# Attention probabilities split in fp16 with three products each, and the softmax maximum taken from the stacked 128-row operands

## The chip, the cores and the metric

The kernel runs on one core of a Trainium2 chip. The metric is the device time of one launch in microseconds (us). TensorE multiplies matrices, VectorE (DVE in the profile), ScalarE (ACT) and GpSimd (POOL) do the element-wise work, and SyncE (SP) issues the transfers (DMA). Every engine runs its own list of instructions in order and waits on semaphores that others raise.

## The reference, cut to what matters

Two layers, each a cross attention followed by a mixture of experts, on x of 2 x 1024 x 256 tokens. The change lies in the first attention alone. There the queries are the layer-normalised x (with 2 x 1024 rows), keys and values come from 77 context rows and the 1024 normalised tokens together:

```
q = latn @ Wq;  kv = concatenate([xn, latn]) @ Wkv      # 16 heads of 64
weight = softmax(einsum('bhld,bhnd->bhln', q * scale, k * scale))
out = einsum('bhln,bhnd->bhld', weight, v);  out @ Wo
```

So for each of 2 batches and 16 heads there are scores of 1024 queries against 1101 keys, an exponential of each, a product with values, and a division by the row's sum.

## The kernel before, in words

Every fp32 quantity that goes into a product is split into an upper part and a remainder, and three products (upper upper, upper remainder, remainder upper) are added.

**Turns and steps.** The first attention works in 16 turns (`turn`, one for a pair of heads, 8 pairs for each of 2 batches). A turn has STEPS = 36 steps: 2 heads x 2 halves of 512 queries x KT = 9 tiles of up to 128 keys. All engines walk through the same steps in their own `turn` functions, and the order of everything in a step is written out by hand.

**A step on TensorE** (`turn`, line 1621) is: the scores of the step three ahead (AHEAD = 3; `scores`, two matmuls of 512 columns, L1582 and L1583, into one of two score banks), and the product of this step's probabilities and values (`attend`, L1602: four groups of 128 queries, with four matmuls of 65 columns each). The scores for a bank need the exponentials of the step two before to be done (s_exp). ScalarE takes one exponential of the 512 columns (L810) into PT, which is fp32. The upper part of a probability is read in place: `upper` takes the upper 16 bits of the fp32 word as bf16. GpSimd (L642) or VectorE (L1104, in the ten VECTOR_STEPS) subtracts it from PT and stores the fp16 remainder PR. `attend` waits for that remainder.

**Stacked operands.** For the scores, Q and K of a head are copied by DMA into stacks: QA holds the upper part of Q twice (2 x 64 rows), KA the upper part and the remainder of K, QB the remainder of Q and a 65th row with minus the maximum of each query, KB the upper part of K and a row of ones. `stack_head` on the SP queue (L505, L508) issues six such transfers for a head, each of about 256 to 276 KB. For head 1 it waits for the first scores of the turn (s_score), for head 0 of the next turn for the last split of the next turn's K (s_jobfree). Each transfer adds 16 to s_stack of its head, so a full stack adds 96.

**The maximum.** The 65th row of QB needs the maximum of each query's scores first. For eight tiles of 128 queries, `max_part` (L1532) makes approximate scores from the upper parts alone: per tile a matmul of 512 keys into the first maximum bank (a = 0, before `attend`), and after `attend` one of 78 and one of 512 keys (a = 1; L1538, L1540). It reads Q and K of the head, 64 rows each, straight from where they were split, not from the stack. VectorE reduces each bank (L1032, L1036); `max_part` waits for the reduction of the tile before (s_mxfree). Then the maxima are joined, turned by TensorE (`max_turn`, M1_T and M0_T), negated, and sent by a small DMA into the row of QB.

**What lies on which step.** Head 1's maxima lie at steps 1 to 8 (M1_AT = 1), head 0's of the next turn at 19 to 26 (M0_AT = 19). Turning the attention output of the turn before lies at steps 1 and 2, its output product at 3 to 6, the projection of the next turn's Q and K (`project_qk`, five jobs) at 13 to 17 (QK_AT = 13). In this text, a step with a tile of maxima is a maximum step; there are 16 in a turn, and 20 plain ones.

**First batch's first head.** Its maxima are taken between the value projections (`values`), which wait for the split of Q and K alone.

Of the kernel before, what the change touches and what calls it, by code (L numbers as in the profile page):

```python
# [7 lines left out]

# [1 line left out]

# [3 lines left out]
P = 128  # L16
ALU = mybir.AluOpType
ACT = mybir.ActivationFunctionType
AX = mybir.AxisListType
F32 = mybir.dt.float32  # L20
F32R = mybir.dt.float32r
U32 = mybir.dt.uint32
BF16 = mybir.dt.bfloat16
F16 = mybir.dt.float16
RMAX = bass.bass_isa.ReduceOp.max

B, T, D = 2, 1024, 256
S = 77
SP = S + 1
NC = D // P  # L30
NT = B * T // P
TB = T // P
HD = 64
PAIRS = 1024 // P
KT = TB + 1
NK = T + SP
NKP = NK + 2
HALF = 512
EPS = 1e-5
STEPS = 4 * KT  # L40
RING = 6
AHEAD = 3
JOBS = 12
VJOBS = 2 * KT
MAX0_T = 2 * TB
BOUND_AT = 9
WQK0_AT = 5
QK0_AT = 9
AWJOBS = 6
# [15 lines left out]
def program(nc, x, ctx, ln1w, ln1b, ln2w, ln2b, wqk0, wv0, wo0, wr, rbias, w1, b1, w2, b2, gb,  # L65
            watt, bqk1, bvo1, wgu, wd, convw, convb, out):
    stack = ExitStack()
    with stack:
# [3 lines left out]
        def sem(name):  # L72
            return stack.enter_context(nc.semaphore(name))
# [3 lines left out]
        score_banks = [ps[:, 0, :], ps[:, 1, :]]  # L77
        max_banks = ps[:, 2:4, :].rearrange("p a n -> p (a n)")
        small_bank = ps[:, 4, :]
# [16 lines left out]
        def sb0(name, shape, dt=F32):  # L96
            return st0.enter_context(nc.sbuf_tensor(name, shape, dt))
# [2 lines left out]
        C = sb0("C", [P, B, D])  # L100
        lnp = sb0("lnp", [P, 4, NC])
        lat = {k: sb0("lat_" + k, [P, B, NC, NKP], F32R) for k in "hl"}
        latf = sb0("latf", [P, 2, HALF])
        wqk_raw = sb0("wqk_raw", [P, NC, 2, P])
        wo_raw = sb0("wo_raw", [P, D])
        wqk = {k: sb0("wqk_" + k, [P, NC, 2, P], F32R) for k in "hl"}
# [1 line left out]
        Q = {k: sb0("Q_" + k, [P, T], F32R) for k in "hl"}  # L108
        K = {k: sb0("K_" + k, [P, NKP], F32R) for k in "hl"}

        QA = [sb0(f"QA{h}", [P, T], F32R) for h in range(2)]
        QB = [sb0(f"QB{h}", [P, T], F32R) for h in range(2)]
        KA = [sb0(f"KA{h}", [P, NKP], F32R) for h in range(2)]
# [2 lines left out]
        V = {k: sb0("V_" + k, [P, KT, 2 * PAIRS, HD + 1], F16) for k in "hl"}  # L116
        PT = sb0("PT", [P, RING, HALF])
        PR = sb0("PR", [P, RING, HALF], F16)
        AT = sb0("AT", [P, TB, P])
        with ExitStack() as early:  # L120
            wv_raw = early.enter_context(nc.sbuf_tensor("wv_raw", [P, NC, KT * P - P], F32))
# [117 lines left out]
        s_wvh = sem("wv_rounded")  # L239
        s_wqk, s_wv, s_wo = sem("wqk_split"), sem("wv_split"), sem("wo_split")  # L240
        s_bounds, s_bound, s_vs = sem("bounds_by_partition"), sem("bounds_ready"), sem("value_scale_ready")
        s_rem_pool, s_rem_dve = sem("remainders_by_gpsimd"), sem("remainders_by_vector")
        s_job = sem("shared_bank_full")
        s_cast = sem("shared_bank_rounded")
# [9 lines left out]
        s_exp = sem("exp_done")  # L254
# [138 lines left out]
            return shared[(1 + idx) % 2]  # L393

        def upper(s):
            return PT[:, s % RING, :].bitcast(BF16).rearrange("p (n two) -> p n two", two=2)[:, :, 1]


        VECTOR_STEPS = (2, 11, 13, 15, 17, 19, 29, 31, 33, 35)

        def on_vector(s):
            return s in VECTOR_STEPS
# [51 lines left out]


        A_AT, WO_AT = 1, 3
        M1_AT, M1_MAX, M1_T = 1, 9, 12
        QK_AT, M0_AT, M0_MAX, M0_T = 13, 19, 27, 29
        WQK_AT, WO_SPLIT_AT = 9, 16

        UNITS = GR * FC
        UP_AHEAD = 2
# [296 lines left out]
        def _(act):  # L759
# [3 lines left out]
                nc.scalar.copy(dst, bk[:, 0:SP] if j == 4 else bk).then_inc(s_cast, 1)  # L763

            act.wait_ge(s_in, 16 * 6)
            for k, (b, c, h) in enumerate(LATJOBS):
                act.wait_ge(s_lat_full, k + 1)
                n = HALF if h < 2 else SP
                w = 2 if h < 2 else 0
                nc.scalar.activation(lat["h"][:, b, c, HALF * h:HALF * h + n], shared[k % 2][:, 0:n], ACT.Identity,  # L770
                                     bias=lnp[:, w + 1, c:c + 1], scale=lnp[:, w, c:c + 1]).then_inc(s_lat_hi, 1)
                if k == WQK0_AT:
                    act.wait_ge(s_wqk_raw, 16)
                    nc.scalar.copy(flat(wqk["h"]), flat(wqk_raw)).then_inc(s_wqk, 1)
                if k >= QK0_AT:
                    round_qk(k - QK0_AT, k - QK0_AT, first_qk_bank(k - QK0_AT))
# [28 lines left out]
            def turn(b, i, g, nb):  # L805
                for s in range(STEPS):
                    m = P if s % KT < TB else S
                    act.wait_ge(s_score, STEPS * g + s + 1)
                    act.wait_ge(s_pv, STEPS * g + s + 1)
                    nc.scalar.activation(PT[0:m, s % RING, :], score_banks[s % 2][0:m], ACT.Exp,  # L810
                                         scale=HD ** -0.5).then_inc(s_exp, 1)
                    at = s - AHEAD
                    if at >= 0 and at % KT == KT - 1:
                        u = at // KT
                        act.wait_ge(s_pv, STEPS * g + at + 1 + RING)
                        act.wait_ge(s_norm, 4 * g + u + 1)
                        nc.scalar.copy(PVS[:, u % 2], pv_bank).then_inc(s_pvc, 1)
                    if A_AT <= at < A_AT + 2:
                        att_hi(jobs_before(b, i), at - A_AT)
                    if nb is not None and QK_AT <= at < QK_AT + 5:  # L820
                        if at == QK_AT:
                            act.wait_ge(s_stack[1], 96 * g + 96)
                        j = at - QK_AT
                        round_qk(j, jobs_before(b, i) + AWJOBS + j, bank(AWJOBS + j))
# [123 lines left out]
        def _(dve):  # L948
# [5 lines left out]
            dve.sem_inc(s_norm, 2)  # L954
            for h in range(2):
                nc.vector.memset(KB[h][HD:HD + 1, :].bitcast(F32), 1.0).then_inc(s_const, 1)
            dve.wait_ge(s_in, 16 * 6)
            dve.wait_ge(s_const, 8)

# [537 lines left out]
        def _(pe):  # L1497
# [34 lines left out]
            def max_part(h, t, a, n):  # L1532

                pe.wait_ge(s_mxfree, 2 * n + a + 1)
                r = slice(HD * h, HD * h + HD)
                q = Q["h"][r, t * P:t * P + P]
                if a == 1:
                    nc.tensor.matmul(small_bank[:, t % 4 * SP:t % 4 * SP + SP], q, K["h"][r, T:NK],  # L1538
                                     start=True, stop=True)
                nc.tensor.matmul(max_banks[:, a * HALF:a * HALF + HALF], q, K["h"][r, a * HALF:a * HALF + HALF],  # L1540
                                 start=True, stop=True).then_inc(s_mx, 1)

            def max_tile(h, t, n):
# [7 lines left out]
            def values(b, job):  # L1551

                for j in range(VJOBS):
                    kt, half = divmod(j, 2)
                    m = P if kt < TB else S
                    pe.wait_ge(s_jobfree, job + j + 1)
                    product(shared[(job + j) % 2][0:m],
                            [(lat[u][:, b, c, kt * P:kt * P + m], wv[v][:, c, HALF * half:HALF * half + HALF])
                             for c in range(NC) for u, v in RANDL]).then_inc(s_job, 1)
                    if b == 0 and half == 0 and kt < TB:  # L1560
                        if kt == 0:
                            pe.wait_ge(s_jobfree, 5 + 2)
                        max_tile(0, kt, kt)
                    if b == 0 and j == MAX0_T:
                        max_turn(0)
# [20 lines left out]
            def attend(g, pair, s):  # L1586
                h, kt = s // (2 * KT), s % KT
                m = P if kt < TB else S
                if on_vector(s):
                    pe.wait_ge(s_rem_dve, len(VECTOR_STEPS) * g + by_vector(s))  # L1590
                else:
                    pe.wait_ge(s_rem_pool, (STEPS - len(VECTOR_STEPS)) * g + s + 1 - by_vector(s))
                if kt == 0:
                    pe.wait_ge(s_pvc, 4 * g + s // KT + 1)
                head = 2 * pair + h
                vh, vl = ((V[k][0:m, kt, head, :] if isinstance(head, int) else
                           V[k][0:m, kt, bass.ds(head, 1), :].squeeze(1)) for k in "hl")
                for q in range(4):
                    c = slice(q * P, q * P + P)
                    for k, (p, v) in enumerate(((upper(s)[0:m, c], vh), (upper(s)[0:m, c], vl),  # L1600
                                                (PR[0:m, s % RING, c], vh), (PR[0:m, s % RING, c], vl))):
                        mm = nc.tensor.matmul(pv_bank[:, q, :], p, v, start=(kt == 0 and q == 0 and k == 0),  # L1602
                                              stop=(kt == KT - 1 and k == 3), skip_group_check=True)
                mm.then_inc(s_pv, 1)

            def att_turn(job, j, bk):
# [14 lines left out]
            def turn(b, i, g, nb):  # L1621
                job = jobs_before(b, i)
                last = i == PAIRS - 1
                for s in range(STEPS):
# [4 lines left out]
                    if M1_AT <= s < M1_AT + TB:  # L1629
                        if s == M1_AT:  # L1630
                            pe.wait_ge(s_maxrow, 2 * g + 1)
                        max_part(1, s - M1_AT, 0, 16 * g + 8 + s - M1_AT)
                    if nb is not None and M0_AT <= s < M0_AT + TB:
                        if s == M0_AT:
                            pe.wait_ge(s_jobfree, job + AWJOBS + 5 + 2)
                            pe.wait_ge(s_maxrow, 2 * g + 2)
                        max_part(0, s - M0_AT, 0, 16 * g + 16 + s - M0_AT)
                    if A_AT <= s < A_AT + 2:
# [401 lines left out]
```

## Time and profile before

| | us |
|---|---|
| three runs | 2375.3, 2377.93 (median), 2394.89 |
| profiled execution | 2373.98 |
| its span, first to last instruction | 2372.3 |
| TensorE matmul busy | 2243.4 (95%) |
| VectorE, GpSimd, ScalarE busy | 1282.3, 1121.8, 728.2 |
| mean granted TensorE clock | 0.949 |

The first attention runs from about 60 us to 1190 us of the span, then the experts of layer 0 to about 1980 us, then layer 1. The busy time of TensorE counts matmuls from start to modelled end, and they overlap, so the distance from one start to the next tells what a matmul costs the engine. A granted clock of 1.00 is 2.4 GHz, and 0.50 is 1.2 GHz.

### The profile page before, as it was taken

How to read it: one execution, taken by the hardware profiler on the slowest of the kernel's cores; microseconds unless marked ns; L12 is line 12 of the kernel's file. 1: busy time of each engine (PE TensorE's matmuls, PEld its weight loads, DVE VectorE, ACT ScalarE, POOL GpSimd, SP SyncE). 2: the span in 40 equal slices, each digit the busy share in tenths (PEclk: the TensorE clock that was granted, in tenths of full speed). 3: DMA queues.
4: the chain of work that ended last, by engine and by line, in shares of the span. 5: the costliest groups of instructions: out<-in, count | busy, mean ns of one | idle time of the engine just before them, and what ended most of it. 6: DMA issues, size and time to landing. Idle time of an engine off the chain costs nothing.

```text
span 2372.3 us, 47010 instructions
## 1 busy us (share of the span) xinstructions
PE 2243.4 (95%) x19460; PEld 1684.1 (71%) x19460; DVE 1282.3 (54%) x2444; ACT 728.2 (31%) x1227; POOL 1121.8 (47%) x1102
## 2 busy tenths in 40 slices
PE   2999999999999999999959999999999997899888
PEld 2666666666666666666639998998998986556567
DVE  8656655666556655565653333333333369535586
ACT  2343333333343344333432222222221221112222
POOL 4144444444335444444536676666665655112132
PEclk9999999999999999999979999999999998657699
DMA  1222222122112222122120000001000000000000
GB/s 63 63 63 45 48 64 58 41 64 63 32 35 64 63 64 62 35 59 64 32 80 19 19 21 34 19 19 37 19 19 19 18 1 0 1 1 1 22 16 27
DMA packets 31026, 87.23 MB, mean 37 GB/s; under 512 B 6820, under 2 KB 13796, under 8 KB 28389
## 3 DMA queue, kind: packets, MB, share of 16 engines
q1 hardware_dynamic: 30820, 84.25, 14.4%
q8 instruction: 158, 2.59, 0.4%
q14 instruction: 48, 0.39, 0.1%
HBM read 29.76 MB, written 2.10 MB: 13 GB/s over the span
## 4 chain that ended last, share of the span: by engine, by line
PE 89%; DVE 6%; issue 1%; ACT 1%; POOL 1%; DMA 0%; POOLq 0%; ACTq 0%; DVEq 0%
PE ps L1504 29%; PE ps L1754 15%; PE ps L1602 13%; PE ps L1582 8%; PE ps L1540 8%; PE ps L1583 6%; PE ps L1846 5%; PE ps L1538 2%; DVE Y L358 1%; PE ps L1609 1%; PE ps L1824 1%; DVE stats L339 1%; PE ps L1694 0%; POOL ln_tmp L376 0%; PE ps L1848 0%
## 5 line engine op out<-in xcount | busy, mean ns | idle before, releaser
L642 POOL TENSOR_TENSOR PR<-PT 128x512 f16<-128x512 f32 (+1 forms) x416 | 445.1, 1072 | 607.0 <-ACT PT L810 606.7
L810 ACT ACTIVATE PT<-ps 128x512 f32<-128x512 f32 (+1 forms) x576 | 344.0, 598 | 537.9 <-PE ps L1583 537.9
L1032 DVE TENSOR_REDUCE mxs<-ps 128x1 f32<-128x512 f32 x512 | 352.3, 689 | 219.9 <-PE ps L1540 219.9
L685 POOL TENSOR_TENSOR h_l<-hf,h_h 128x512 fp32r<-128x512 f32 x256 | 336.4, 1315 | 244.6 <-DVE hf L1206 238.6
L1206 DVE TENSOR_SCALAR hf<-ps,b1e 128x512 f32<-128x512 f32 x256 | 191.7, 750 | 447.0 <-ACT h_h L882 446.2
L882 ACT ACTIVATE h_h<-ps,b1e 128x512 fp32r<-128x512 f32 x256 | 176.0, 688 | 563.0 <-PE ps L1504 562.9
L1602 PE MATMUL ps<-V_h,PT 128*128 128x65 f16 (+1 forms) x2304 | 329.7, 197 | 5.0 <-POOL PR L642 4.0
L1602 PEld LDWEIGHTS ps<-V_h,PT 128*128 128x128 bf16 (+1 forms) x2304 | 225.5, 98 | 150.2 <-issue 134.9
L1602 PE MATMUL ps<-V_l,PT 128*128 128x65 f16 (+1 forms) x2304 | 324.1, 194 | 0.0
L1602 PE MATMUL ps<-V_l,PR 128*128 128x65 f16 (+1 forms) x2304 | 321.9, 194 | 0.0
L1602 PE MATMUL ps<-V_h,PR 128*128 128x65 f16 (+1 forms) x2304 | 321.4, 193 | 0.0
L1754 PE MATMUL ps<-w_h,h_h 128*128 128x256 f32 x1024 | 291.6, 285 | 3.1 <-POOL h_l L685 3.0
L1754 PE MATMUL ps<-w_l,h_h 128*128 128x256 f32 x1024 | 290.1, 283 | 0.0
L1754 PE MATMUL ps<-w_h,h_l 128*128 128x256 f32 x1024 | 290.1, 283 | 0.0
L1582 PE MATMUL ps<-QA,KA 128*128 128x512 f32 (+1 forms) x576 | 273.9, 476 | 2.6 <-DMA QB<-maxT 2.1
L1540 PE MATMUL ps<-K_h,Q_h 64*128 64x512 f32 x512 | 248.1, 486 | 0.0
L1602 PEld LDWEIGHTS ps<-V_l,PT 128*128 128x128 bf16 (+1 forms) x2304 | 227.7, 99 | 0.4
L1583 PE MATMUL ps<-QB,KB 65*128 65x512 f32 (+1 forms) x576 | 227.9, 396 | 0.0
L1602 PEld LDWEIGHTS ps<-V_h,PR 128*128 128x128 f16 (+1 forms) x2304 | 226.5, 98 | 0.0
L1602 PEld LDWEIGHTS ps<-V_l,PR 128*128 128x128 f16 (+1 forms) x2304 | 224.7, 98 | 0.0
L1504 PE MATMUL ps<-XT_h,w_h 128*128 128x512 f32 x512 | 203.1, 397 | 7.1 <-DVE hf L1206 4.7
L1754 PEld LDWEIGHTS ps<-w_h,h_h 128*128 128x128 f32 x1024 | 195.7, 191 | 17.3 <-POOL h_l L685 4.1
(307 smaller groups left out, 4560.2 us busy)
## 6 DMA issues: line engine op xcount, KB each, us to landing
QA<-Q_h SPq DMA_DIRECT2D x64, 256.0 KB, 3.4
w_raw<-w SPq DMA_DIRECT2D x16, 1024.0 KB, 4.8
KA<-K_h SPq DMA_DIRECT2D x32, 275.5 KB, 5.2
KA<-K_l SPq DMA_DIRECT2D x32, 275.5 KB, 5.4
KB<-K_h SPq DMA_DIRECT2D x32, 275.5 KB, 5.6
QB<-Q_l SPq DMA_DIRECT2D x32, 256.0 KB, 4.3
wqk_raw<-wqk SPq DMA_DIRECT2D x16, 256.0 KB, 3.9
wo_raw<-wo SPq DMA_DIRECT2D x18, 128.0 KB, 4.5
```

Of the source, the lines that this page charges most:

```text
L642: nc.gpsimd.tensor_tensor(PR[0:m, s % RING, :], PT[0:m, s % RING, :], upper(s)[0:m], ALU.subtract).then_inc(s_rem_pool, 1)
L685: nc.gpsimd.tensor_tensor(hs["l"][:, u % 4], hf[:, u % 2], hs["h"][:, u % 4].bitcast(F32), ALU.subtract).then_inc(s_hlo, 1)
L810: nc.scalar.activation(PT[0:m, s % RING, :], score_banks[s % 2][0:m], ACT.Exp, scale=HD ** -0.5).then_inc(s_exp, 1)
L882: nc.scalar.activation(hs["h"][:, u % 4], hidden_banks[u % 2], ACT.Relu, bias=b1e[:, k, u % FC:u % FC + 1]).then_inc(s_hhi, 1)
L1032: r = nc.vector.reduce_max(mxs[:, a, t:t + 1], max_banks[:, a * HALF:a * HALF + HALF], AX.X)
L1206: nc.vector.tensor_scalar(hf[:, u % 2], hidden_banks[u % 2], b1e[:, k, u % FC:u % FC + 1], 0.0, ALU.add, ALU.max).then_inc(s_hf, 1)
L1504: mm = nc.tensor.matmul(o, l, r, start=(k == 0), stop=(k == n - 1), **kw)
L1540: nc.tensor.matmul(max_banks[:, a * HALF:a * HALF + HALF], q, K["h"][r, a * HALF:a * HALF + HALF], start=True, stop=True).then_inc(s_mx, 1)
L1582: nc.tensor.matmul(o, KA[h][:, k], QA[h][:, q], start=True, stop=False)
L1583: nc.tensor.matmul(o, KB[h][0:HD + 1, k], QB[h][0:HD + 1, q], start=False, stop=True) \
L1602: mm = nc.tensor.matmul(pv_bank[:, q, :], p, v, start=(kt == 0 and q == 0 and k == 0), stop=(kt == KT - 1 and k == 3), skip_group_check=True)
L1754: mm = nc.tensor.matmul(o, hs[a][:, u % 4, t * P:t * P + P], w2s[b][:, k, f, :], start=(f == 0 and j == 0 and t % 2 == 0), stop=(f == FC - ...
```

## The change

- The exponential is multiplied by 1024 (a bias `lift` = 10 ln 2, read from a column of SBUF), and is taken twice by ScalarE from the same score bank: once as fp32 into PT, once as fp16 into a new buffer PU. `upper` returns PU. The semaphore for "exponential done" is raised by the second.
- `attend` drops the product of the remainder of the probabilities with the remainder of the values: three matmuls for each of the four groups, not four.
- `max_part` reads QA and KA of the head, 128 rows, not 64 rows of Q and K. It therefore waits for the stack: head 1's first tile for s_stack[1], head 0's for s_stack[0] of the next turn, and the one in `values` for the first stack of all.
- Places move: the maxima of head 1 from steps 1-8 to 3-10, their turn from 12 to 13, the projections of the next turn from 13-17 to 10-14, the split of their weights on GpSimd from step 9 to 7; head 0's maxima stay at 19-26. VECTOR_STEPS has ten entries as before, at other places.

```diff
-MAX0_T = 2 * TB
+MAX0_T = 2 * TB + 1
...
         def upper(s):
-            return PT[:, s % RING, :].bitcast(BF16).rearrange("p (n two) -> p n two", two=2)[:, :, 1]
-        VECTOR_STEPS = (2, 11, 13, 15, 17, 19, 29, 31, 33, 35)
+            return PU[:, s % RING, :]
+        VECTOR_STEPS = (2, 14, 16, 18, 19, 20, 30, 32, 34, 35)
...
-        M1_AT, M1_MAX, M1_T = 1, 9, 12
-        QK_AT, M0_AT, M0_MAX, M0_T = 13, 19, 27, 29
-        WQK_AT, WO_SPLIT_AT = 9, 16
+        M1_AT, M1_MAX, M1_T = 3, 11, 13
+        QK_AT, M0_AT, M0_MAX, M0_T = 10, 19, 27, 29
+        WQK_AT, WO_SPLIT_AT = 7, 16
...
                     nc.scalar.activation(PT[0:m, s % RING, :], score_banks[s % 2][0:m], ACT.Exp,
-                                         scale=HD ** -0.5).then_inc(s_exp, 1)
+                                         bias=lift[0:m, 0:1], scale=HD ** -0.5)
+                    nc.scalar.activation(PU[0:m, s % RING, :], score_banks[s % 2][0:m], ACT.Exp,
+                                         bias=lift[0:m, 0:1], scale=HD ** -0.5).then_inc(s_exp, 1)
...
                 pe.wait_ge(s_mxfree, 2 * n + a + 1)
-                r = slice(HD * h, HD * h + HD)
-                q = Q["h"][r, t * P:t * P + P]
+                q = QA[h][:, t * P:t * P + P]
                 if a == 1:
-                    nc.tensor.matmul(small_bank[:, t % 4 * SP:t % 4 * SP + SP], q, K["h"][r, T:NK],
+                    nc.tensor.matmul(small_bank[:, t % 4 * SP:t % 4 * SP + SP], q, KA[h][:, T:NK],
                                      start=True, stop=True)
-                nc.tensor.matmul(max_banks[:, a * HALF:a * HALF + HALF], q, K["h"][r, a * HALF:a * HALF + HALF],
+                nc.tensor.matmul(max_banks[:, a * HALF:a * HALF + HALF], q, KA[h][:, a * HALF:a * HALF + HALF],
                                  start=True, stop=True).then_inc(s_mx, 1)
...
                         if kt == 0:
-                            pe.wait_ge(s_jobfree, 5 + 2)
+                            pe.wait_ge(s_stack[0], 96)
...
                     for k, (p, v) in enumerate(((upper(s)[0:m, c], vh), (upper(s)[0:m, c], vl),
-                                                (PR[0:m, s % RING, c], vh), (PR[0:m, s % RING, c], vl))):
+                                                (PR[0:m, s % RING, c], vh))):
...
                         if s == M1_AT:
                             pe.wait_ge(s_maxrow, 2 * g + 1)
+                            pe.wait_ge(s_stack[1], 96 * g + 96)
...
                         if s == M0_AT:
-                            pe.wait_ge(s_jobfree, job + AWJOBS + 5 + 2)
+                            pe.wait_ge(s_stack[0], 96 * g + 192)
```

## Rows read from the trace of the kernel before

**Rows 1.** The page: granted clock in 40 slices of the span, and VectorE's reductions.
```profile
PEclk9999999999999999999979999999999998657699
...
L1032 DVE TENSOR_REDUCE mxs<-ps 128x1 f32<-128x512 f32 x512 | 352.3, 689 | 219.9 <-PE ps L1540 219.9
```

**Rows 2.** Timeline of TensorE's matmuls, a plain step: start us, duration us, instruction.
```profile
339.76 0.48 PE L1582 MATMUL ps<-QA,KA 128*128 128x512 f32 x1
340.08 0.40 PE L1583 MATMUL ps<-QB,KB 65*128 65x512 f32 x1
340.32 0.21 PE L1602 MATMUL ps<-V_h,PT 128*128 128x65 f16 x1
...
340.82 0.48 PE L1582 MATMUL ps<-QA,KA 128*128 128x512 f32 x1
```

**Rows 3.** Timeline of TensorE's matmuls, a maximum step of head 0.
```profile
343.05 0.50 PE L1582 MATMUL ps<-QA,KA 128*128 128x512 f32 x1
343.38 0.39 PE L1583 MATMUL ps<-QB,KB 65*128 65x512 f32 x1
343.70 0.50 PE L1540 MATMUL ps<-K_h,Q_h 64*128 64x512 f32 x1
344.13 0.21 PE L1602 MATMUL ps<-V_h,PT 128*128 128x65 f16 x1
...
344.73 0.30 PE L1538 MATMUL ps<-K_h,Q_h 64*128 64x78 f32 x1
344.86 0.48 PE L1540 MATMUL ps<-K_h,Q_h 64*128 64x512 f32 x1
345.27 0.50 PE L1582 MATMUL ps<-QA,KA 128*128 128x512 f32 x1
```

**Rows 4.** Timeline of TensorE's matmuls, 128-row products behind one another.
```profile
335.70 0.39 PE L1582 MATMUL ps<-QA,KA 128*128 128x512 f32 x1
335.93 0.39 PE L1583 MATMUL ps<-QB,KB 65*128 65x512 f32 x1
...
338.13 0.39 PE L1582 MATMUL ps<-QA,KA 128*128 128x512 f32 x1
...
339.65 0.28 PE L1504 MATMUL ps<-lat_h,wqk_l 128*128 128x78 f32 x1
```

**Rows 5.** Timeline of ScalarE: exponentials, a cast, an activation with a bias column.
```profile
308.37 0.60 ACT L810 ACTIVATE PT<-ps 128x512 f32<-128x512 f32 x1 [1.11 <-PE ps L1583]
311.39 0.60 ACT L810 ACTIVATE PT<-ps 128x512 f32<-128x512 f32 x1 [2.42 <-PE ps L1583]
...
335.90 0.59 ACT L763 CAST K_h<-ps 128x512 fp32r<-128x512 f32 x1 [1.35 <-PE ps L1504]
336.38 0.60 ACT L810 ACTIVATE PT<-ps 128x512 f32<-128x512 f32 x1
...
1890.56 0.69 ACT L882 ACTIVATE h_h<-ps,b1e 128x512 fp32r<-128x512 f32 x1 [2.47 <-PE ps L1504]
1891.14 0.61 ACT L887 CAST wa_h<-w_raw 128x512 fp32r<-128x512 f32 x1
```

**Rows 6.** Timeline of the SP queue: stacks of heads 1, 0 and 1.
```profile
298.52 1.11 SPq L505 DMA_DIRECT2D QA<-Q_h  x2
...
340.50 1.14 SPq L505 DMA_DIRECT2D QA<-Q_h  x2
...
344.88 1.40 SPq L508 DMA_DIRECT2D KB<-K_h  x1
...
365.66 1.11 SPq L505 DMA_DIRECT2D QA<-Q_h  x2
```

**Rows 7.** Instructions on tile KB, 290 to 440 us: from issue to landing.
```profile
DMA to landing us min/median/max: 5.3/5.7/5.8
```

**Rows 8.** Timeline of TensorE's first value projection after a stop.
```profile
59.77 0.47 PE L1504 MATMUL ps<-wv_h,lat_h 128*128 128x512 f32 x1 [3.61 <-DVE K_l L980]
...
60.71 0.63 PE L1504 MATMUL ps<-wv_h,lat_h 128*128 128x512 f32 x1
61.13 0.63 PE L1504 MATMUL ps<-wv_l,lat_h 128*128 128x512 f32 x1
```

**Rows 9.** The stretch after it: each engine's busy us, granted clock (0.53), DMA.
```profile
60.00:67.20 7.20, 6.75 (x16) 4.17 (x16) 2.91 (x9) 1.38 (x2) 0.37 (x1) 0.53 0.86 178
```

More of the change, by code:

```diff
@@ L11 @@
+import math
 from contextlib import ExitStack
@@ L40 @@
 STEPS = 4 * KT
+LIFT = 10 * math.log(2.0)
 RING = 6
@@ L102, in program @@
         lat = {k: sb0("lat_" + k, [P, B, NC, NKP], F32R) for k in "hl"}
-        latf = sb0("latf", [P, 2, HALF])
+        with ExitStack() as early:
+            latf = early.enter_context(nc.sbuf_tensor("latf", [P, 2, HALF], F32))
+        PU = sb0("PU", [P, RING, HALF], F16)
         wqk_raw = sb0("wqk_raw", [P, NC, 2, P])
@@ L118, in program @@
         PR = sb0("PR", [P, RING, HALF], F16)
+        lift = sb0("lift", [P, 1])
         AT = sb0("AT", [P, TB, P])
@@ L241, in program @@
         s_bounds, s_bound, s_vs = sem("bounds_by_partition"), sem("bounds_ready"), sem("value_scale_ready")
+        s_lift = sem("exponent_lift_ready")
         s_rem_pool, s_rem_dve = sem("remainders_by_gpsimd"), sem("remainders_by_vector")
@@ L765, in _ @@
             act.wait_ge(s_in, 16 * 6)
+            act.wait_ge(s_lift, 1)
             for k, (b, c, h) in enumerate(LATJOBS):
@@ L956, in _ @@
                 nc.vector.memset(KB[h][HD:HD + 1, :].bitcast(F32), 1.0).then_inc(s_const, 1)
+            nc.vector.memset(lift[:], LIFT).then_inc(s_lift, 1)
             dve.wait_ge(s_in, 16 * 6)
@@ L1600, in attend @@
                     for k, (p, v) in enumerate(((upper(s)[0:m, c], vh), (upper(s)[0:m, c], vl),
-                                                (PR[0:m, s % RING, c], vh), (PR[0:m, s % RING, c], vl))):
+                                                (PR[0:m, s % RING, c], vh))):
                         mm = nc.tensor.matmul(pv_bank[:, q, :], p, v, start=(kt == 0 and q == 0 and k == 0),
-                                              stop=(kt == KT - 1 and k == 3), skip_group_check=True)
+                                              stop=(kt == KT - 1 and k == 2), skip_group_check=True)
                 mm.then_inc(s_pv, 1)
```

## The prediction

> **What bounds it now.** I read the page first: TensorE is busy 95% of the span, and in the first attention, slices 2 to 20, its granted clock stays at or near full (2.4 GHz) [rows 1]. Then TensorE's timeline, start to start. A plain step is 1.06 us, from the first score matmul to the next step's: 0.32, 0.24, and 0.50 for 16 matmuls of 65 columns, 0.031 each [rows 2]. A maximum step is 2.22 [rows 3], and there a matmul with 64 rows is dear: 0.43 until the next start before the values (343.70 to 344.13), 0.41 before the scores, while a 128-row one of 512 columns behind its like costs 0.23 [rows 4]. ScalarE's timeline shows it waiting for scores before most exponentials [rows 5]. The SP queue gives the period: a turn is 365.66 - 298.52 = 67.14 us [rows 6]. TensorE's own order of work is thus the bound, with nearly no waits.
>
> **The dropped product.** 4 matmuls of 0.031 less make 0.12 us a step, if TensorE sets the step [rows 2].
>
> **The 128-row maximum.** In a maximum step, old to new, by rows 3 against rows 2 and 4: scores to a = 0, 0.32 to 0.23; that to the values, 0.43 to 0.24; values to the 78 columns, 0.12 to 0.03; those to a = 1, 0.13 to 0.11; that to the scores, 0.41 to 0.23; first to second score matmul, 0.33 to 0.23. That is 1.74 to 1.07, 0.67 less, and with the dropped products 0.79 less: 2.22 falls to about 1.45 (I keep 0.02 for rounding). With 12 value matmuls instead of 16 counted from zero the sum is 1.40, the lower bound. The upper bound, where each of the three pairs of 512 columns costs the 0.32 of rows 2 and not 0.23, is 1.65. VectorE needs two reductions of 0.69 in such a step [rows 1], which still fits, though at the fourth tile and beside the output additions it will be late; by its order of work I add 0.8 us a turn at steps 7-8 and 0.3 at 22-23, estimates from that 0.69.
>
> The Trainium skill (TensorEngine Tiling (Array Packing), Key Properties) says that changing between tiling modes drains the array. Here the 64-row matmuls pay on entry and on exit [rows 3], so the trace agrees in kind; the page has no number.
>
> **The second exponential.** Without a bias column the exponential takes 0.60 us; an activation with one takes 0.69, and the next starts 0.58 after it [rows 5]. Two of them make 1.17 us a step on ScalarE, more than TensorE's 1.06 - 0.12 = 0.94 in a plain step. So a plain step gets longer, 1.06 to 1.17, and the 0.12 gained there is lost. Bounds: 1.06 (nothing lost) and 1.27 (two full 0.60 plus handing over). In a maximum step (1.45) ScalarE fits. The copies of the product bank come behind both exponentials, which costs about 0.4 us where ScalarE is full.
>
> The Trainium skill (ScalarE: Activation LUTs, What ACT_TABLE_LOAD costs) states 93 ns for each pointer operand and 93 ns of overlap back to back; the trace agrees (0.69 against 0.60, 0.58 apart). By its figures the pair would come to about 1.23 us.
>
> **The new waits.** This is what matters most. A stack is six transfers issued one behind another: head 0's begins at 340.50, its last is issued at 344.88 and lands 5.3 to 5.8 later, so 9.7 to 10.2 after the trigger by that reading [rows 6, 7]; I take 9.8. Nothing waited for that before: the stack was needed only by the scores of the next turn. Now TensorE stands in its queue at two places in each turn, and with it the scores, value products and everything behind.
>
> *Head 0, step 19.* The trigger is the last split of K, 0.74 us after the start of the step behind the last projection (339.76 to 340.50) [rows 2, 6], about 0.1 more with the doubled exponentials. That step is now 15. The stack is there 10.65 us after it begins. TensorE reaches the wait after four plain steps, 4 x 1.17, a copy of 0.4 and its scores of 0.56: 5.6 us. It stands 5.0 us.
>
> *Head 1, step 3.* The trigger is the first score of the turn, computed in step 33 of the turn before: its second matmul ends 0.72 us in (340.08 + 0.40 - 339.76) [rows 2], and I add 0.04 for the hand-over. The stack lands 10.56 us after step 33 begins. TensorE needs steps 33 to 35 at 1.17, step 0 at 1.3, steps 1 and 2 at 1.45 (0.94 and an estimated 0.5 for the turning of the output), and 0.56: 8.3. It stands 2.3 us.
>
> **A turn added up.**
> - Step 33 to the first maximum of step 3: 10.56.
> - Steps 3-10: four with an output product, 3.02 before [rows 5], 2.25 now; four at 1.45; less 0.56 already counted; VectorE 0.8; a projection, 2.43 - 1.05 = 1.38 (335.70 to 338.13) [rows 4]. Sum 16.4.
> - Steps 11-14: three at 2.43 - 0.12, one at 1.6 (its projection has 78 columns). 8.5.
> - Step 15 to the first maximum of step 19: 10.65.
> - Steps 19-26: 8 x 1.45 less 0.56, plus 0.3: 11.3.
> - Steps 27-32: 6 x 1.17 and a copy of the bank: 7.5.
>
> Together 64.9 us, against 67.14.
>
> **The clock.** Behind a stop of 3.61 us TensorE ran the next 7 us at a granted clock of 0.53, that is mostly at 1.2 GHz, and a matmul of 512 columns cost 0.42 and not 0.23 [rows 8, 9]. The stop of 5.0 us should sometimes do that. Bounds: nothing, and 7 us at 0.23/0.42, which loses 3.2. I take the middle, 1.6. A turn is then 66.5 us, 0.64 less than before.
>
> **The sum.** 15 turns have both waits: -9.6. The last one has no step-19 wait but also no maxima of head 0, -1. The first maxima, in the value projection, wait for a stack that is triggered as that projection starts (59.77, a place of its own in rows 8): some 7.5 us of standing, less 8 x 0.4 saved, +4. The first turn of each batch comes to step 3 about 1.7 us earlier after its trigger than the others, +3. GpSimd's subtraction, the move of its weight split to step 7 and VectorE's vector steps I cost at nothing: they lie under the steps of 1.17 us and more and under the two stops; if that cover fails it is one subtraction a place. The lift column costs nothing to speak of. Total -4 on the profiled 2374: **2370 us**, and the runs' median stands 4 us above the profiled execution, so the comparison with 2378 is no other case.
>
> **Rival 1: the stacks arrive in time (faster).** If a stack were usable one landing time after its trigger (5.7) and the issues did not line up, step 3 would not wait and step 19 about 0.9 us: 64.9 - 2.3 - 4.1 = 58.5 a turn, 15 x 8.6 = 130 us less, with the terms outside near **2250**. For it: the gain of TensorE is real, some 9 us a turn. Against it: SP is seen issuing the six over 5.8 us [rows 6]. In between lie cases in which TensorE's path is shorter than I think elsewhere, or no stop ever lowers the clock (2345).
>
> **Rival 2: the stops throw the array to its low clock (slower).** The mechanism has one place, the stretch behind steps 3 and 19, and one price, up to 3.2 us each. If both always pay, a turn is 71.3 us, 15 x 4.2 = 62 more, and with the terms outside near **2440**. A turn is slower than before once the clock costs more than 2.2 us in it. For it: rows 8 and 9, and slices of the page in the last part with a clock of 5 or 6 although TensorE has work [rows 1]. Against it: the 2.3 us stop is shorter than the one seen, and behind each there is dense work.
>
> The Trainium skill (TensorE: Matmul & The Clock Gate, Why this matters for your kernels) warns that an idle gap between bursts of matmuls sends the clock back to half. By that rule alone step 19 would pay every time: rival 2 in part. The trace shows one such stop in the same direction.
>
> **Rival 3: the matmul's cost is in the 512 columns, not in the 64 rows.** Then maximum steps stay at 2.1, and a turn is 75 us, near 2490. Rows 4 speak against it.
>
> **How the numbers follow.** A measurement of this kernel tells from no change what is over 1% away, below 2354 or above 2402. The forecast has 0.60, with a range of its own from 2330 to 2415 (clock 0 to 3.2 a turn, maximum steps 1.40 to 1.65, plain steps 1.06 to 1.27, landing 9.3 to 10.2); of it 0.15 lies under 2354, 0.40 between, 0.05 above. Rival 1 with its halves has 0.19, rival 2 has 0.17, rival 3 and the rest 0.04. So faster 0.34, within 1% 0.40, slower 0.26. The range leaves out the far half of rival 1 and the end of rival 2: 2280 to 2425.
>
> **What would show it.** In the changed profile: exponentials in pairs 0.58 apart of 0.69 each; maximum steps of about 1.45; plain steps of 1.17; TensorE idle before the first maximum of a head, about 5 us at step 19 and 2 at step 3, released by the DMA into KB; a granted clock that dips inside the first attention. The forecast is wrong if these stops are missing, if the stack lands earlier than 9 us, or if the steps behind a stop run at double length.

## The result and the profile after

The changed kernel takes 2424.94 us (median of 4 runs, 2422.36 to 2428.31); the kernel before took 2385.92 in the same comparison (4 runs, 2375.30 to 2394.89). It got slower: each of its runs lies above each run of before. The two medians are 1.6% apart; the ratio on record, taken over the fast runs of both, is 1.0217 with a 95% interval of 1.018 to 1.0253. 2370 was forecast, and the result lies at the very top of the range (2280 to 2425). The profiled execution took 2425.43 us, with a span of 2423.7 and a mean granted clock of 0.908; before, 2373.98, 2372.3 and 0.949.

The page of the changed kernel, its clock in 40 slices and four groups of instructions (busy us, mean ns of one, idle before them and what ended it):

```profile
PEclk9898899989898998999988999999999999657789
...
L817 ACT ACTIVATE PT<-ps,lift 128x512 f32<-128x512 f32 (+1 forms) x576 | 405.7, 704 | 301.0 <-PE ps L1592 299.6
L1042 DVE TENSOR_REDUCE mxs<-ps 128x1 f32<-128x512 f32 x512 | 349.4, 689 | 223.6 <-PE ps L1549 208.9
...
L819 ACT ACTIVATE PU<-ps,lift 128x512 f16<-128x512 f32 (+1 forms) x576 | 403.6, 701 | 0.0
L1549 PE MATMUL ps<-KA,QA 128*128 128x512 f32 x512 | 250.9, 492 | 128.1 <-DMA KB<-K_h 79.1
```

Against [rows 1] two things are new. The first attention (slices 2 to 20) is no longer at full clock: slices of 8 stand between the 9s. And the maximum's matmuls (L1549) have 128.1 us of idle time before them, most of it ended by the DMA into KB. VectorE's reductions (L1042) are what they were, 689 ns and as many.

TensorE's waits of the changed kernel from 200 to 620 us of the span, 6.0 turns (us in total, times, longest):

```profile
PE ps L1549 <- DMA KB<-K_h: 28.9, 6, 5.3
PE ps L1549 <- issue: 17.9, 6, 3.7
```

The same view of the kernel before shows no such wait. Here are six stops of 4.8 us and six of 3.0 on the mean: the first kind is step 19, the second step 3. The second kind is put down to "issue", which means that the profile shows no releaser for it; SP's rows for such a stop, further below, say what it is.

One step-19 stop, in the order of time, SP's queue first (QA to KB are the six transfers of the stack), then TensorE (idle in brackets):

```profile
422.33 1.13 SPq L511 DMA_DIRECT2D QA<-Q_h  x2
423.50 0.60 SPq L511 DMA_DIRECT2D QB<-Q_l  x1
424.15 1.22 SPq L514 DMA_DIRECT2D KA<-K_h  x1
425.41 1.22 SPq L514 DMA_DIRECT2D KA<-K_l  x1
426.68 1.42 SPq L514 DMA_DIRECT2D KB<-K_h  x1
```

```profile
421.48 0.47 PE L1591 MATMUL ps<-QA,KA 128*128 128x512 f32 x1
...
426.58 0.47 PE L1591 MATMUL ps<-QA,KA 128*128 128x512 f32 x1
426.89 0.39 PE L1592 MATMUL ps<-QB,KB 65*128 65x512 f32 x1
432.23 0.80 PE L1549 MATMUL ps<-KA,QA 128*128 128x512 f32 x1 [4.95 <-DMA KB<-K_h]
432.83 0.28 PE L1611 MATMUL ps<-V_h,PU 128*128 128x65 f16 x1
...
433.73 0.77 PE L1549 MATMUL ps<-KA,QA 128*128 128x512 f32 x1
434.31 0.63 PE L1591 MATMUL ps<-QA,KA 128*128 128x512 f32 x1
434.73 0.63 PE L1592 MATMUL ps<-QB,KB 65*128 65x512 f32 x1
...
436.60 0.40 PE L1591 MATMUL ps<-QA,KA 128*128 128x512 f32 x1
436.84 0.40 PE L1592 MATMUL ps<-QB,KB 65*128 65x512 f32 x1
437.07 0.39 PE L1549 MATMUL ps<-KA,QA 128*128 128x512 f32 x1
```

Step 15 begins at 421.48, step 19 at 426.58. The last of six transfers is issued at 426.68 and TensorE starts at 432.23, 5.55 later and 9.90 after the first issue. Behind the stop a matmul of 512 columns takes 0.42 to the next start, and from 436.60 on 0.23: the array runs at 1.2 GHz for some 4 us and then at 2.4 again.

Seven us of the time in which the stack moves (columns as in [rows 9]: the last three are the granted clock, the share of the DMA engines that is busy, and GB/s):

```profile
424.00:431.00 7.00, 2.46 (x30) 1.39 (x28) 2.17 (x5) 4.51 (x9) 2.31 (x2) 0.87 0.98 205
```

The DMA engines are busy nearly all of the time. The six transfers are 1.63 MB, and at 205 GB/s that is 8 of the 9.9 us (an estimate). Before the change they ran at much the same rate (0.97 busy and 201 GB/s from 342 to 347 us), and nobody waited.

A step-3 stop of the turn before: the first and the last issue of head 1's stack on the SP queue, then TensorE's timeline:

```profile
316.00 1.12 SPq L511 DMA_DIRECT2D QA<-Q_h  x2
...
320.31 1.36 SPq L514 DMA_DIRECT2D KB<-K_h  x1
```

```profile
322.86 0.39 PE L1592 MATMUL ps<-QB,KB 65*128 65x512 f32 x1
326.20 0.47 PE L1549 MATMUL ps<-KA,QA 128*128 128x512 f32 x1 [2.96 <-issue]
...
326.77 0.20 PE L1611 MATMUL ps<-V_h,PR 128*128 128x65 f16 x1
326.80 0.23 PE L1611 MATMUL ps<-V_h,PU 128*128 128x65 f16 x1
326.83 0.25 PE L1611 MATMUL ps<-V_l,PU 128*128 128x65 f16 x1
...
329.01 0.63 PE L1591 MATMUL ps<-QA,KA 128*128 128x512 f32 x1
329.44 0.63 PE L1592 MATMUL ps<-QB,KB 65*128 65x512 f32 x1
```

The stop is 2.96 us. It ends 10.20 after the first issue and 5.89 after the last, so it ends with the same landing as the other kind. TensorE starts again at full speed, and 0.6 us later, with work at hand, it falls to half.

The stretches around the step-19 stop: length, busy us of TensorE, its weight loads, VectorE, ScalarE and GpSimd, then the granted clock, the DMA share and GB/s:

```profile
426.90:432.20 5.30, 0.38 (x2) 0.00 (x0) 0.24 (x1) 1.61 (x3) 2.31 (x2) 0.72 0.84 177
432.20:436.30 4.10, 4.07 (x32) 3.05 (x32) 1.86 (x3) 0.90 (x2) 0.00 (x0) 0.53 0.00 0
436.30:440.95 4.65, 4.57 (x54) 3.27 (x52) 4.12 (x8) 3.56 (x7) 3.15 (x3) 1.00 0.00 0
```

The clock is 0.72 on the mean within the stop, so it fell before the stop had ended; that part of the low clock costs nothing.

ScalarE in the plain steps ahead of it, the exponentials in pairs:

```profile
422.22 0.69 ACT L817 ACTIVATE PT<-ps,lift 128x512 f32<-128x512 f32 x1 [0.19 <-PE ps L1592]
422.81 0.68 ACT L819 ACTIVATE PU<-ps,lift 128x512 f16<-128x512 f32 x1
423.38 0.69 ACT L817 ACTIVATE PT<-ps,lift 128x512 f32<-128x512 f32 x1
423.95 0.70 ACT L819 ACTIVATE PU<-ps,lift 128x512 f16<-128x512 f32 x1
424.52 0.71 ACT L817 ACTIVATE PT<-ps,lift 128x512 f32<-128x512 f32 x1
```

They are 0.57 apart and a plain step is 1.15, against 1.06 in [rows 2].

Below, a turn is taken apart into its 36 steps, each from its first score matmul to the next step's, as means over turns 1 to 6 and 9 to 14 (those away from a batch's beginning and end). Step 31 is a plain one. All in us; the last column is the turn:

```
kernel              step 31  step 3  step 4  steps 5,6  step 19  step 20  steps 21,22  turn
before               1.05    3.01    3.00    5.95       2.20     2.22     4.43         66.92
changed              1.15    6.97    2.88    4.42       7.66     2.57     3.17         69.68
```

Summed over the 15 intervals between the stacks of head 1, the turns take 1081.0 us against 1040.4. That is 40.6 of the 51.4 us by which the span grew. Ahead of them are 7.2 (the first stack of head 1 is issued at 106.37, before at 99.22), behind them 3.6, of which 2.3 are in the last turn, which has the step-3 stop too.

### The profile page after: what moved, and what is told of

It reads as the page before. It is cut to its first block, busy times and chain, and to the rows that moved or that the text cites. A ratio compares the mean times of both kernels' runs of the same rounds, so it can differ in the third digit from the quotient of the medians.

```text
span 2423.7 us, 42979 instructions
## 1 busy us (share of the span) xinstructions
PE 2136.3 (88%) x17156; PEld 1670.9 (69%) x17156; DVE 1292.3 (53%) x2445; ACT 1079.2 (45%) x1803; POOL 1160.2 (48%) x1102
## 4 chain that ended last, share of the span: by engine, by line
PE 71%; DVE 8%; ACT 6%; issue 5%; DMA 4%; SPq 3%; POOL 1%; POOLq 0%; ACTq 0%; DVEq 0%
PE ps L1514 29%; PE ps L1764 15%; PE ps L1549 6%; PE ps L1611 6%; PE ps L1856 4%; PE ps L1591 4%; DMA KB<-K_h 4%; PE ps L1592 3%; ACT PT L817 3%; ACT PU L819 2%; SPq L514 2%; DVE mxs L1042 1%; SPq L511 1%; PE ps L1547 1%; DVE Y L364 1%
## 5 line engine op out<-in xcount | busy, mean ns | idle before, releaser
L648 POOL TENSOR_TENSOR PR<-PT,PU 128x512 f16<-128x512 f32 (+1 forms) x416 | 482.1, 1161 | 616.7 <-ACT PU L819 616.7
L817 ACT ACTIVATE PT<-ps,lift 128x512 f32<-128x512 f32 (+1 forms) x576 | 405.7, 704 | 301.0 <-PE ps L1592 299.6
L1042 DVE TENSOR_REDUCE mxs<-ps 128x1 f32<-128x512 f32 x512 | 349.4, 689 | 223.6 <-PE ps L1549 208.9
L819 ACT ACTIVATE PU<-ps,lift 128x512 f16<-128x512 f32 (+1 forms) x576 | 403.6, 701 | 0.0
L1549 PE MATMUL ps<-KA,QA 128*128 128x512 f32 x512 | 250.9, 492 | 128.1 <-DMA KB<-K_h 79.1
L1611 PEld LDWEIGHTS ps<-V_h,PU 128*128 128x128 f16 (+1 forms) x2304 | 217.6, 101 | 181.5 <-issue 127.3
L1611 PE MATMUL ps<-V_h,PU 128*128 128x65 f16 (+1 forms) x2304 | 290.8, 201 | 22.2 <-ACT PVS L826 15.5
L1611 PE MATMUL ps<-V_l,PU 128*128 128x65 f16 (+1 forms) x2304 | 284.6, 199 | 0.0
L1611 PE MATMUL ps<-V_h,PR 128*128 128x65 f16 (+1 forms) x2304 | 282.4, 198 | 0.0
L1611 PEld LDWEIGHTS ps<-V_l,PU 128*128 128x128 f16 (+1 forms) x2304 | 224.6, 102 | 0.5
L1549 PEld LDWEIGHTS ps<-KA,QA 128*128 128x128 f32 x512 | 109.2, 213 | 162.1 <-DMA KB<-K_h 87.1
```

Source lines behind the costliest of these rows:

```text
L648: nc.gpsimd.tensor_tensor(PR[0:m, s % RING, :], PT[0:m, s % RING, :], upper(s)[0:m], ALU.subtract).then_inc(s_rem_pool, 1)
L819: nc.scalar.activation(PU[0:m, s % RING, :], score_banks[s % 2][0:m], ACT.Exp, bias=lift[0:m, 0:1], scale=HD ** -0.5).then_inc(s_exp, 1)
L1042: r = nc.vector.reduce_max(mxs[:, a, t:t + 1], max_banks[:, a * HALF:a * HALF + HALF], AX.X)
```

## The experiments

Theory: the maximum on 128 rows saves what was forecast, and two things eat it, the wait for the six transfers and the clock that falls behind each of the two stops. Rival A: the products' half of the change (the second exponential) is what costs. Rival B: the stop itself is the whole price, and the half clock behind it costs nothing that counts.

**e1_products, the products' half alone.** The maximum, its places in the order and its operands are those of before; the two exponentials and the three products stay.

```diff
-                q = QA[h][:, t * P:t * P + P]
+                r = slice(HD * h, HD * h + HD)
+                q = Q["h"][r, t * P:t * P + P]
...
-                            pe.wait_ge(s_stack[1], 96 * g + 96)
```

> The products' half alone: two exponentials with the bias, fp16 upper part, three products; the maximum on 64 rows, its waits and all places of steps as before. Theory (the stops for the stack and the low clock behind them made the change slow): no stop and no dip of the clock; plain steps 1.16 us for 1.05, the 22 other steps 0.12 shorter, a turn near 65.7 us for 66.9, in all about 2355 us, a ratio to before of 0.99. Rival (the doubled exponential on ScalarE is what costs): a turn over 68 us and a time above 2400.

Measured: 2379.99 (2378.69 to 2398.69), ratio 1.0016 [0.9964, 1.0069], so no change. The steady turn came out as expected, 65.62. The total did not: the first turn took 83 us. Two stretches of the same time in the two traces, first this kernel, then the kernel before (columns as above):

```profile
100.00:105.00 5.00, 3.68 (x21) 2.24 (x20) 0.69 (x1) 4.53 (x8) 2.32 (x2) 0.78 0.71 151
105.00:148.00 43.00, 43.00 (x230) 26.98 (x229) 17.64 (x30) 16.72 (x28) 13.84 (x12) 0.51 0.13 31
148.00:155.00 7.00, 7.00 (x65) 5.31 (x65) 2.90 (x4) 5.36 (x10) 3.35 (x4) 1.00 0.01 3
```

```profile
105.00:148.00 43.00, 43.00 (x456) 29.48 (x456) 25.65 (x45) 15.78 (x29) 19.36 (x19) 1.00 0.27 59
```

TensorE has no gap in these 43 us in either kernel, and does 230 matmuls at a clock of 0.51 against 456 at 1.00. (This kernel has 12 value matmuls in a step and the other 16, so the counts are not quite of the same work.) By the turns, that stretch is worth some 18 us (83.3 less 65.6). Rival A falls: the half gains 1.3 us a turn.

**e2_rows128, the maximum's half alone.** One exponential without a bias column, the upper part by bits as before, four products; the new maximum and both waits stay.

```diff
-            return PU[:, s % RING, :]
+            return PT[:, s % RING, :].bitcast(BF16).rearrange("p (n two) -> p n two", two=2)[:, :, 1]
...
+                                                (PR[0:m, s % RING, c], vh), (PR[0:m, s % RING, c], vl))):
```

> The maximum's half alone: stacked 128-row operands, their waits and the moved places of steps; one exponential without bias, bf16 upper part, four products as before. Theory: both stops and the low clock are there as in the changed kernel; steps that TensorE sets are 0.12 us longer than in it, plain ones 0.1 shorter; a turn about 71 us, in all about 2445 us. Rival (the second exponential costs): below 2400 us.

Measured: 2442.35 (2441.90 to 2445.30), ratio 1.0263 [1.022, 1.0305]. TensorE's waits from 200 to 620 us:

```profile
PE ps L1547 <- DMA KB<-K_h: 33.0, 6, 5.6
PE ps L1547 <- issue: 16.8, 6, 3.0
```

The stops are there, 5.5 and 2.8 us on the mean: the first is longer by 0.7, about what steps 15 to 18 before it have become shorter (0.8). The turn is 71.15, 4.2 above before. The two halves add up: -1.3 and +4.2 make +2.9, and the whole change has +2.8. The loss is the maximum's.

**e3_no_stack_wait.** The changed kernel, with the maximum's 128 rows read from Q_h and K_h themselves, both heads together, which needs no transfer.

```diff
-                q = QA[h][:, t * P:t * P + P]
+                q = Q["h"][:, t * P:t * P + P]
...
-                            pe.wait_ge(s_stack[1], 96 * g + 96)
```

> The changed kernel, but the maximum's matmuls read the 128 rows of the split Q and K of both heads, which need no transfer, so the waits for the stack go (the waits of before take their place). The maxima are then those of the sum over both heads, not of one head. Theory: both stops and all dips of the clock in the first attention vanish, maximum steps stay at 1.50 us; a turn is about 57 us, in all about 2225 us. Rival (64-row to 128-row makes no difference in cost, or ScalarE bounds the turn): a turn over 63 us, above 2310.

Measured: 2236.79 (three of four runs from 2236.50 to 2238.41; before 2375.87), turn 57.46, expected 57. TensorE does matmuls of the same number and shapes, and only the operands and the waits differ, so waiting and what follows from it cost 12.2 us a turn, 69.68 less 57.46. The fourth run took 2194.36, at a clock of 0.968 where the others had 0.942.

**e4_fill, the clock apart from the stop.** The changed kernel, with matmuls that nobody reads (13 ahead of the wait of step 3, 20 ahead of that of step 19). The stops last as long; the array is not idle in them.

```diff
+            def fill(n, count):
+                pe.wait_ge(s_mxfree, 2 * n + 1)
+                for _ in range(count):
+                    nc.tensor.matmul(max_banks[:, 0:HALF], lat["h"][:, 0, 0, 0:P], lat["h"][:, 0, 0, 0:HALF], ...)
...
+                            fill(16 * g + 8, 13)
...
+                            fill(16 * g + 16, 20)
```

> The changed kernel with matmuls of 128x512 without use ahead of the two waits (13 at step 3, 20 at step 19, into the first maximum bank, about 3 and 4.6 us of work at full clock), so that TensorE is at work while the stack lands. Theory (the low clock behind the stops costs 4.6 us a turn): the first maxima come at the same time behind the trigger, steps 4 and 20 take 2.2 and 1.5 us instead of 2.9 and 2.6, the granted clock stays at 1.00 through the turns; in all about 2360 us. Rival (the steps behind a stop are long for VectorE's or the queue's sake, not the clock's): no gain, 2425 or more.

Measured: 2371.66 (2369.79 to 2381.74), ratio to before 0.9972 [0.9927, 1.0016], and 53 us under the changed kernel. TensorE's timeline around step 19:

```profile
345.46 0.40 PE L1599 MATMUL ps<-QB,KB 65*128 65x512 f32 x1
345.70 4.74 PE L1556 MATMUL ps<-lat_h 128*128 128x512 f32 x20
350.74 0.50 PE L1549 MATMUL ps<-KA,QA 128*128 128x512 f32 x1 [0.30 <-DMA KB<-K_h]
...
352.12 0.39 PE L1599 MATMUL ps<-QB,KB 65*128 65x512 f32 x1
352.35 0.39 PE L1549 MATMUL ps<-KA,QA 128*128 128x512 f32 x1
```

TensorE still goes on only when the transfer has landed, 5.3 us after its scores, but the next matmuls cost 0.23. Steps of the two kernels:

```
kernel              step 3  step 4  step 19  step 20  step 21  turn
changed              6.97    2.88    7.66     2.57     1.66    69.68
with filling         5.61    2.20    6.86     1.51     1.51    65.62
```

The clock costs 4.06 us a turn: 2.04 behind the stop of 3 us and 2.01 behind that of 5. Rival B falls, and what is left of waiting is 65.62 less 57.46, 8.2 us.

**e5_order, fewer transfers ahead of the maximum.** The maximum reads QA and KA only. These four transfers go first and count on a semaphore of their own; QB and KB follow.

```diff
-                for dst, src in ((QA[h][0:HD], Q["h"][r]), (QA[h][HD:P], Q["h"][r]), (QB[h][0:HD], Q["l"][r])):
-                    sp.dma_start(dst.bitcast(F32), src.bitcast(F32)).then_inc(s_stack[h], 16)
+                for dst, src in ((QA[h][0:HD], Q["h"][r]), (QA[h][HD:P], Q["h"][r]),
+                                 (KA[h][0:HD, 0:NK], K["h"][r, 0:NK]), (KA[h][HD:P, 0:NK], K["l"][r, 0:NK])):
+                    sp.dma_start(dst.bitcast(F32), src.bitcast(F32)).then_inc(s_top[h], 16)
...
-                            pe.wait_ge(s_stack[1], 96 * g + 96)
+                            pe.wait_ge(s_top[1], 64 * g + 64)
```

> The changed kernel with the six transfers of a stack in another order and under two semaphores: the two of QA and the two of KA first, and the maximum waits for those four alone; the scores still wait for all six. Theory (the stops are as long as the transfers that are waited for): the first maximum comes about 7 us behind the trigger instead of 9.8, both stops are 2.8 us shorter, and the low clock behind them mostly goes; a turn about 61 us, in all near 2300 us. Rival (the transfers share the bandwidth, so that all land together): no change, 2425.

Measured: 2308.16 (2302.82 to 2309.19), turn 61.86. The kernel before took 2375.28 (median of 7 runs) in this and the next three comparisons. TensorE's waits, 200 to 620 us:

```profile
PE ps L1552 <- DMA KA<-K_l: 13.7, 7, 2.2
...
PE ps L1552 <- issue: 0.5, 1, 0.5
```

Step 3 falls from 6.97 to 2.46, step 19 from 7.66 to 4.67. The stop of step 3 is gone, that of step 19 is 2 us, and its step 20 still costs 2.64 instead of 1.51: even a stop of about 2 us is followed by half clock here. The rival (no change) falls. But the four are also two thirds of the bytes, so this run does not tell whether the order of the issues or the rate of the DMA engines sets the time.

**v1_padded, the gain without the wait.** 128 rows need no stacks: K_h holds both heads in its 128 rows, and a copy of Q_h with zeros in the other head's rows (QZ) gives one head's product. VectorE writes QZ.

```diff
+                nc.vector.memset(QZ[HD - HD * h:P - HD * h, :].bitcast(F32), 0.0).then_inc(s_qz, 1)
...
+                nc.vector.tensor_copy(QZ[r, cols], Q["h"][r, cols].bitcast(F32)).then_inc(s_qz, 1)
...
-                q = QA[h][:, t * P:t * P + P]
+                q = QZ[:, t * P:t * P + P]
```

> The changed kernel with the maximum on 128 rows, but from a Q that VectorE copies into one more buffer with zeros in the rows of the other head, against the 128 rows of K's upper part: no transfer is waited for, and the maxima are those of the reference's head. VectorE does five more copies or fills a turn. Theory: as with the waits gone, a turn near 57.5 us, in all 2195 to 2240 us. Rival (VectorE's extra work lies on the path): a turn over 60 us, above 2280.

Measured: 2242.08 (2241.98 to 2243.25), turn 57.33, as e3 to 0.1 us. VectorE's copies cost nothing that shows.

**v2_padded_lift_in_row.** v1, with the constant that the bias column adds put into the row of negated maxima instead, in the instruction of VectorE that makes this row anyway. The exponentials have no bias column then.

```diff
-                                         bias=lift[0:m, 0:1], scale=HD ** -0.5)
+                                         scale=HD ** -0.5)
...
-                nc.vector.tensor_scalar(maxT[h][:], small_bank[0:TB, 0:P], -1.0, None, ALU.mult).then_inc(s_maxrow, 1)
+                nc.vector.tensor_scalar(maxT[h][:], small_bank[0:TB, 0:P], -1.0, LIFT * HD ** 0.5,
+                                        ALU.mult, ALU.add).then_inc(s_maxrow, 1)
```

> The padded version (v1_padded) with the lift added to the row of negated maxima by VectorE's existing instruction, so that the two exponentials need no bias column. Theory (the bias column costs 0.09 us an exponential, and the pair sets the plain steps): exponentials of 0.60, a pair takes 0.97 and not 1.17 us, plain steps 1.00 for 1.16; a turn near 55.5 us, 30 us less in all than v1_padded. Rival (plain steps are bound by the way from scores to exponentials and back, not by ScalarE's own time): 1.07 or more for a plain step and under 15 us less.

Measured: **2210.92** (2207.89 to 2222.08), a ratio of the medians to before of 0.931, and no run of one lies within 100 us of a run of the other; 31 us under v1. Its exponentials, and a plain step of TensorE:

```profile
330.34 0.62 ACT L822 ACTIVATE PU<-ps 128x512 f16<-128x512 f32 x1
330.82 0.63 ACT L820 ACTIVATE PT<-ps 128x512 f32<-128x512 f32 x1
331.29 0.64 ACT L822 ACTIVATE PU<-ps 128x512 f16<-128x512 f32 x1
```

```profile
330.03 0.50 PE L1617 MATMUL ps<-QA,KA 128*128 128x512 f32 x1
330.36 0.39 PE L1618 MATMUL ps<-QB,KB 65*128 65x512 f32 x1
331.01 0.50 PE L1617 MATMUL ps<-QA,KA 128*128 128x512 f32 x1
```

A pair is 0.96 us and the mean plain step 0.97 (0.98 here), and ScalarE's rows have no idle time: ScalarE sets the step, by 0.03 over the 0.94 that the prediction gave TensorE. The turn is 55.25.

**v3_padded_one_exp.** v1, with the one exponential, the upper part and the four products of before.

```diff
-                    nc.scalar.activation(PU[0:m, s % RING, :], score_banks[s % 2][0:m], ACT.Exp,
-                                         bias=lift[0:m, 0:1], scale=HD ** -0.5).then_inc(s_exp, 1)
+                                         scale=HD ** -0.5).then_inc(s_exp, 1)
```

> The padded maximum with the products of before: one exponential without bias, the bf16 upper part read in place, four products. Theory: plain steps 1.05 us, steps that TensorE sets 0.12 longer than in v1_padded; a turn near 58.6 us, about 18 us more in all than v1_padded. Rival (the second exponential costs as much as the fourth product saves): equal to v1_padded.

Measured: 2245.54 (2243.50 to 2255.22), turn 57.95. Against v1 that is 3.5 us, less than the 18 expected: with a bias column the fp16 half is worth 0.6 us a turn, and only without the column (v2) 2.7. (By the turns, 0.6 would be 9 us in all; why the whole shows only 3.5 was not traced.) Of the 9.6 us a turn that v1 gains over before, 9.0 come from the maximum.

## Why the prediction was wrong

**The step that failed is the clock term.** It was set at 1.6 us a turn, the middle between nothing and 3.2, and measures 4.06. The bounds were drawn around one stop only; the three-microsecond stop of step 3 was given no price at all, since it is shorter than the one of [rows 8]. Both pay, 2.04 and 2.01. The price of a single fall was not too low: 7 us of work at half clock were taken for a stop [rows 9], and about 4 are seen, the rest of the low clock lying within the longer stop. What was wrong is "sometimes" and "one": all 30 such stops of the trace, 15 at step 3 and 15 at step 19, are followed by work at half clock. 2.46 us a turn over 15 turns is 37 of the 55 us by which the forecast missed. The prediction itself said that a turn is slower than before once the clock costs over 2.2 us in it.

The Trainium skill (TensorE: Matmul & The Clock Gate, Why this matters for your kernels) warns of idle gaps between bursts of matmuls, and here the rows agree with it more fully than I used it: it was read as bearing on step 19 alone.

This is rival 2 in its mechanism. Its price was too high (3.2 where 2.0 was paid), which other terms partly made up for, so the result lies at 2425 and not at 2440. It had 0.17, and the rows for it were in the text: one stop in the trace, one fall of the clock. A mechanism that had acted at the one stop shown was the likelier case, and the middle of its bounds was no case at all.

**The placing of the stops was right.** Head 0: from the start of step 15 to the first maximum 10.65 was worked out, 10.75 is read above (10.6 to 11.1 over the turns); the wait is reached after 5.80 (10.75 less the stop), 5.6 was taken; the stop 5.0, measured 4.95. The stack takes 9.90 from its first issue, 9.8 was taken. Head 1: 10.56 against a median of 10.85 (10.75 to 11.94; over 11.5 in four turns); reached after some 8.0 where 8.3 was taken, so the stop is 3.0 and not 2.3. That the whole group of six decides it, and not one landing time, is shown by e5, where four of them in front take 4.5 us off step 3. What the prediction gave as the reason, the issues one behind another, is open: the DMA engines are 0.98 busy meanwhile, and the bytes alone take about as long.

**The steps on TensorE and ScalarE were right.** The pair of exponentials 1.15 (1.17 taken), the maximum step 1.50 (1.45), steps 5 and 6 at 2.20 to 2.22 (2.25). e4's turn, nearly without a fall of the clock, is 65.62 against the 64.9 worked out; head 0's maximum steps take 0.7 more and the two stretches up to the first maxima 0.7 more, while steps 27 to 32 take 0.8 less. VectorE's lateness, 0.8 at steps 7 and 8 and 0.3 at steps 22 and 23, measures 0.7 and 0.3. Over 15 turns the 0.7 are 10 us more of the miss. Another 3 us come from the turn before: 67.14 was read from one turn, and the mean is 66.92. The dropped product and the second exponential together are worth -1.3 us a turn (e1), the rest +4.2 (e2). One bound of the sum was added up wrong: three pairs at 0.32 and not 0.23 put 0.27 on 1.40 or 1.45, which is 1.67 to 1.72 and not 1.65; the 1.50 measured does not depend on it.

**The work outside the turns** was set at +6 (4, 3 and -1) and is 10.8. The first maxima in the value projection take 7.2 instead of 4: the stop is 7.83 us, and behind it the value matmuls start 0.43 apart for some 4 us. The last turn was set at 1 less and takes 2.3 more, since it has the step-3 stop and the clock behind it. The 3 us for a batch's first turn are not seen: the first turn of all grew by 0.7 us and that of the second batch by 2.4, the others by 2.8. Together this is 5 us more of the miss.

**Rival 1** is refuted for the change as made, and its 58.5 a turn is close to what the kernel does once nothing waits for transfers (57.46, e3). **Rival 3** is refuted by the 1.50 of the maximum steps, with the same 512 columns.

What stays open: what put the array at half clock for 43 us in e1's first turn, with no gap in its work; and why one run of e3 and one of the kernel before (2333.39 us, where the others have 2374 to 2395) are some 42 us shorter. That it is the stretch of low clock late in the span (the slices of 5 to 7 in every page) that these two runs lack fits the clock of 0.968, but neither was profiled.

## What to carry to other kernels

A wait placed on the busy engine costs its own length and then the clock: price both, at every place where it occurs, and take a mechanism that the trace shows once as the case, not as half a case. When an operand is to be widened for the sake of the array, look for one that needs no transfer (zeros in the other head's rows and a copy by an engine that has time) before moving the wait. And count the transfers, and the bytes, that one wait covers, and look at the DMA share of the stretch: a wait on the first four of six (e5) took 4.5 us off step 3 and 3.0 off step 19.

## What the runs showed of the hardware

- A stop of TensorE of 3.0 us costs as much afterwards as one of 5.0 (2.04 and 2.01 us of lost work in some 4 us at 1.2 GHz, by e4), and one of 2 us was still followed by half clock (e5, step 20 at 2.64 against 1.51). In the longer stop a part of the low clock lies within the stop itself (0.72 on the mean there). The fall may come after the array has restarted: 0.6 us later in the rows of step 3 above. It may also come ahead of the stop: in 3 of the 15 step-19 stops the score matmuls just before it are already 0.57 apart and not 0.32, behind a wait of 0.79 us for the copy of the product bank (the granted clock is 0.50 from 358.08 us on, at the start of one of these steps).
- Matmuls that nobody reads keep the clock up. 33 of them a turn are worth 4.06 us a turn, 53 us in all (e4).
- Six transfers on one SP queue, 1.63 MB from SBUF to SBUF, keep the DMA engines 0.98 busy at 205 GB/s and are there 9.9 us after the first issue, though each single one lands 3.3 to 5.8 us after its own.
- Continuous work does not always bring the clock back: 43 us at 0.51 without a gap (e1), in which 230 matmuls were done and not 456.
- A bias column costs 0.19 us for two exponentials in a row (a pair is 1.15 with it, 0.96 without), 2.1 us a turn and 31 us in all (v2 against v1). The Trainium skill (ScalarE: Activation LUTs, What ACT_TABLE_LOAD costs) states 93 ns for each pointer operand; the runs agree, 0.095 for one. The pair worked out from its figures, an estimate of 1.23 us, is more than the 1.15 measured.
